# Accumulating the last two layers in the output tensor, with a reordered start and a changed end: a fused block on 8 cores

## Chip, cores, metric

The kernel runs on the 8 cores of one Trainium2 chip (two dies, cores 0 to 3 and 4 to 7). Each core works on 1,024 of the 8,192 tokens, with no traffic between cores. The metric is the device time of the slowest core in microseconds (us).

## What is computed

```python
xn = layernorm(x)                                   # x: 8192 x 2048, f32
a  = (xn @ W_in.T)[:, :4096];  z = silu((xn @ W_in.T)[:, 4096:])
a  = a @ conv_w.T                                   # 4096 x 4096
attn = ((a * D) * z) @ W_out.T                      # -> 2048
h  = relu(xn @ W1.T + b1);  h = relu(h @ W2.T + b2) # 4096, 4096
out = x + attn + (h @ W3.T + b3)                    # 8192 x 2048, f32
```

`W_x`, `W_dt` and `b_dt` of the reference feed nothing that reaches the output.

## The kernel before

Every matrix product is split into a 2 by 2 grid of blocks and is done with seven block products in place of eight (products 5, 2, 1, 3, 4, 6, 7 in that order), whose operands are sums and differences of blocks. VectorE (DVE) forms these sums of weights (`w_sum`, `o_sum`) and of activations (`f_sum`, `new_forms`, `tile_form`), and combines the products, which TensorE (PE) leaves in PSUM. ScalarE (ACT) takes snapshots of PSUM and applies the nonlinearities. GpSimd (POOL) issues the stores and part of the loads, SyncE (SP) the loads of X and of the weights. Each engine has one list of instructions in a fixed order (`Line.do`), with waits on semaphores (`Line.need`).

There are five feature-major layers (`FM`: WX, WZ, W1, WC, W2), 16 pairs of output blocks each (index `g` from 0 to 79), whose results go through DRAM tensors X1S, ZS, H1S, GS, H2S. Then come two token-major layers (`TM`: WO with `si` 0 and W3 with `si` 1), in four chunks of columns each (`x` from 0 to 7). A chunk has the seven products, each in two halves `u` (32 matmuls of 128x256), and gives eight output pieces of 256 tokens by 256 columns (`items`, `n` from 0 to 63): products 3, 4, 6 and 7, two halves each. `o_close(n)` finishes a piece on DVE into one of six ring slots of 256 KB, and `r_store(n)` has POOL store it.

**The residual.** During the first layer POOL loads X tile by tile with `xb_load` (the last load is L526, that of b3 is L522), adds b3 with `xb_add` (L532, 8 tiles) and stores the sum as `XB` (L534). In the WO layer `r_load(n)` (L898, POOL) brings the piece of XB into the ring slot, four pieces ahead (`PREF`), `o_close` adds the product to it, and the sum is stored to `PS`. The W3 layer does the same with PS as its input and OUT as its output. Pieces of products 3 and 4 take one DVE operation (L929). Pieces of products 6 and 7 take two: bank plus running sum (L935), and then plus the loaded piece (L937). The next products in the same PSUM banks wait for these. The first `r_load`s wait for the last store of H2S, since ring and staging buffers share memory.

**The start.** Eight token tiles are normalised (`S`: statistics on DVE L313/L316, `R`: reciprocal deviation on ACT L322/L325, `N` on DVE L335 or `N_act` on ACT L358), transposed on PE (`transposes`, L377, 16 blocks of 128x128 per tile in two PSUM banks `q`), and evacuated (`E`, ACT L398 or DVE L395). Tile 6 is normalised on DVE. PE's order at the end of the start is: transposes of tile 6, the 8 matmuls of `product((0,2))`, transposes of tile 7, `product((0,5))`, `product((1,2))`, `product((1,5))`.

**The end.** The last piece (n = 63) goes through L935 and L937, its store is issued by POOL (L905), POOL waits for the last six stores, and the program closes (L127).

Of the kernel before, what the change touches and what calls it, by code (L numbers as in the profile page):

```python
# [22 lines left out]
CW = 256  # L23

# [21 lines left out]
    dict(w="WO", src="GS", res="XB", dst="PS"),  # L46
    dict(w="W3", src="H2S", res="PS", dst="OUT"),
# [35 lines left out]
def build_program():  # L83
# [17 lines left out]
    for name in ("XB", "PS"):  # L101
        dram[name] = nc.dram_tensor(name, [TC, HID], F32, kind="Internal")
# [19 lines left out]
    c_bs = [ctr(f"bs{i}") for i in range(2)]  # L122
    c_b3 = ctr("b3")
    c_rl = [ctr(f"rl{i}") for i in range(6)]
    c_rs = [ctr(f"rs{i}") for i in range(6)]

    with ExitStack() as ctx:  # L127
# [401 lines left out]
        def xb_add(j):  # L529
            i = j % 2  # L530
            pool.need(tk_bs["b3"], tk_bs[("l", j)])
            t = pool.do(lambda e: e.tensor_tensor(f_f32(4, i), f_f32(4, i), f_f32(5, 0), ALU.add), c_pool)  # L532
            pool.need(t)
            tk_bs[j] = pool.do(lambda e: e.dma_start(dram["XB"][j * 128:(j + 1) * 128, :], f_f32(4, i)),  # L534
                               c_bs[i], 16)
# [171 lines left out]
        for g in range(NG):  # L707
# [435 lines left out]
```

How the kernel before makes its waits and increments, by code:

```python
    def need(self, *toks):  # L65
        for t in toks:
            if t is None:
                continue
            c, v = t
            if self.met.get(c, 0) < v:
                self.met[c] = v
                self.ops.append(lambda e, c=c, v=v: e.wait_ge(c.h, v))
# [1 line left out]
    def do(self, fn, c=None, n=1):  # L74
        if c is None:
            self.ops.append(fn)
            return None
        c.v += n
        self.ops.append(lambda e: fn(e).then_inc(c.h, n))
        return (c, c.v)
```

## Time and profile before

| | us |
|---|---|
| device time, median of 3 runs (1804.3 to 1806.08) | 1805.95 |
| device time of the profiled execution | 1810.24 |
| its span on the slowest core (core 4) | 1808.6 |
| spans of cores 0 to 7 | 1804.3, 1799.3, 1804.9, 1799.2, 1808.6, 1797.7, 1799.1, 1804.1 |
| PE busy on core 4 | 1760.8 |
| DVE, ACT, POOL busy on core 4 | 900.4, 229.1, 212.6 |

A span runs from a core's first instruction to its last. The device time of the profiled execution is 1.6 us more than the longest span. PEld is the loading of weights into PE, which overlaps the matmuls. A wait is put down to what came last before the waiting instruction went on.

### The profile page before, as it was taken

The numbers are of one execution on the slowest core, as the hardware profiler recorded it, in microseconds if no ns is written. First come the engines' busy times: TensorE is split into PE (matmuls) and PEld (weight loads), VectorE is DVE, ScalarE is ACT, GpSimd is POOL, SyncE is SP. The second block draws the span as 40 slices with busy tenths as digits, with TensorE's granted clock in tenths as the row PEclk, the third lists the DMA queues.
The fourth block names the chain that finished last, engine by engine and source line by source line (L and its number), as shares of the span: only waits on it lengthen the run. The fifth ranks groups of instructions, "written<-read, shape, count | busy, mean of one in ns | idle before, by whom it ended". The sixth has DMA issues, their size and how long they took to land.

```text
span 1808.6 us, 24736 instructions; the slowest of 8 cores (1797.7 to 1808.6 us)
## 1 busy us (share of the span) xinstructions
PE 1760.8 (97%) x9911; PEld 977.2 (54%) x9984; DVE 900.4 (50%) x1137; ACT 229.1 (13%) x355; POOL 212.6 (12%) x265
## 2 busy tenths in 40 slices
PE   3999999999999999999999999999999999999998
PEld 2444444444444444444444444444445788888887
DVE  7744444444444674444444743333333654466443
ACT  4111122222222200000000011111111000000000
POOL 0123220000000000000000000000000122212221
PEclk8999999999999999999999999999999999999999
DMA  9566653333347534333345733223337755885532
GB/s 290 179 231 210 229 182 136 140 134 112 139 146 263 172 118 140 127 113 118 132 140 183 259 117 107 91 97 113 117 117 244 224 191 176 268 261 187 166 115 71
DMA packets 58015, 296.33 MB, mean 164 GB/s; under 512 B 7600, under 2 KB 7600, under 8 KB 40368
## 3 DMA queue, kind: packets, MB, share of 16 engines
q1 hardware_dynamic: 29376, 167.79, 28.9%
q0 software_dynamic: 28240, 126.89, 19.7%
q8 instruction: 81, 1.33, 0.3%
q14 instruction: 30, 0.25, 0.0%
q10 hardware_dynamic: 288, 0.08, 0.0%
HBM read 227.62 MB, written 67.11 MB: 163 GB/s over the span
## 4 chain that ended last, share of the span: by engine, by line
PE 90%; DVE 4%; DMA 3%; issue 1%; POOL 0%; ACT 0%; DVEq 0%; SPq 0%; POOLq 0%; ACTq 0%
PE ps L293 72%; PE ps L867 18%; DVE sF L240 2%; DMA sM<-XB 1%; DVE sST L313 1%; DVE sW L240 1%; DMA PS<-sM 1%; DMA H2S<-sM 1%; DMA sF<-X 1%; POOL sM L898 0%; PE ps L377 0%; DVE sM L335 0%; DVE sM L584 0%; DVE sM L562 0%; DVE sM L929 0%
## 5 line engine op out<-in xcount | busy, mean ns | idle before, releaser
L293 PE MATMUL ps<-sF,sW 128*128 128x512 bf16 (+1 forms) x6199 | 1352.7, 379 | 5.7 <-ACT sF L398 0.8
L293 PEld LDWEIGHTS ps<-sF,sW 128*128 128x128 f16 x6272 | 613.6, 98 | 743.4 <-issue 6.2
L240 DVE TENSOR_TENSOR sW<-sW 128x1024 f16<-128x1024 f16 (+1 forms) x480 | 442.6, 954 | 174.5 <-DMA sW<-W 129.8
L867 PE MATMUL ps<-sW,sF 128*128 128x256 f16 x3584 | 394.5, 273 | 6.3 <-DVE sM L929 3.0
L867 PEld LDWEIGHTS ps<-sW,sF 128*128 128x128 bf16 x3584 | 351.0, 98 | 49.9 <-issue 8.3
L557 DVE TENSOR_TENSOR sM<-ps,sM 128x512 f32<-128x512 f32 x80 | 55.4, 692 | 321.1 <-ACT sM L552 321.1
L613 DVE TENSOR_TENSOR sM<-ps,sM 128x512 f32<-128x512 f32 (+1 forms) x160 | 110.2, 690 | 118.8 <-PE ps L293 118.6
L552 ACT ACTIVATE sM<-ps 128x512 f32<-128x512 f32 x80 | 47.8, 598 | 602.6 <-PE ps L293 579.0
L240 DVE TENSOR_TENSOR sF<-sF 128x2048 bf16<-128x2048 bf16 (+2 forms) x94 | 104.3, 1176 | 0.5 <-DMA sF<-H1S 0.5
L594 ACT ACTIVATE sM<-sM,sCN 128x512 bf16<-128x512 f32 x64 | 46.2, 724 | 243.0 <-DVE sM L613 242.9
L562 DVE TENSOR_TENSOR sM<-ps,sM 128x512 f32<-128x512 f32 x80 | 55.0, 688 | 22.9 <-PE ps L293 22.9
L584 DVE SCALAR_TENSOR_TENSOR sM<-ps,sCN,sM 128x512 bf16<-128x512 f32 x32 | 23.9, 751 | 68.2 <-PE ps L293 68.2
L594 ACT ACTIVATE sM<-ps,sCN 128x512 bf16<-128x512 f32 x64 | 44.1, 689 | 104.6 <-PE ps L293 104.5
L625 POOL DMA_DIRECT2D H2S<-sM x16 | 11.5, 717 | 364.9 <-ACT sM L594 364.9
L625 POOL DMA_DIRECT2D GS<-sM x16 | 11.6, 726 | 351.0 <-DVE sM L584 351.0
L911 ACT ACTIVATE sM<-ps 128x512 f32<-128x512 f32 x16 | 9.5, 598 | 339.1 <-PE ps L867 339.0
L929 DVE TENSOR_TENSOR sM<-ps,sM 128x512 f32<-128x512 f32 x32 | 21.8, 690 | 45.2 <-PE ps L867 41.0
L377 PE MATMUL ps<-sID,sM 128*128 128x128 bf16 x128 | 14.4, 300 | 28.0 <-DVE sM L335 26.9
L916 DVE TENSOR_TENSOR sM<-ps,sM 128x512 f32<-128x512 f32 x16 | 10.9, 691 | 61.2 <-ACT sM L911 61.2
L905 POOL DMA_DIRECT2D OUT<-sM x32 | 22.9, 715 | 140.8 <-DVE sM L929 107.0
L532 POOL TENSOR_TENSOR sF<-sF 128x2048 f32<-128x2048 f32 x8 | 36.7, 4583 | 2.7 <-DMA sF<-X 2.7
L905 POOL DMA_DIRECT2D PS<-sM x32 | 22.9, 715 | 108.5 <-DVE sM L929 86.2
(38 smaller groups left out, 316.4 us busy)
## 6 DMA issues: line engine op xcount, KB each, us to landing
sW<-W SPq DMA_DIRECT2D x48, 1024.0 KB, 8.3
sW<-WC SPq DMA_DIRECT2D x32, 1024.0 KB, 8.1
sW<-WX SPq DMA_DIRECT2D x32, 512.0 KB, 6.4
sW<-WZ SPq DMA_DIRECT2D x32, 512.0 KB, 4.7
sW<-W SPq DMA_DIRECT2D x32, 512.0 KB, 4.5
sW<-WO SPq DMA_DIRECT2D x16, 1024.0 KB, 8.2
X1S<-sM POOLq DMA_DIRECT2D x16, 512.0 KB, 6.3
sF<-X POOLq DMA_DIRECT2D x8, 1024.0 KB, 8.8
```

The lines of the kernel that those rows point to most:

```text
L240: return line.do(lambda e: e.tensor_tensor(out, a, b, ALU.subtract if sub else ALU.add), c)
L293: return e.matmul(ps[bank][:], sW[:, c0 + k * 128:c0 + (k + 1) * 128], rhs[:, k * TH:(k + 1) * TH], start=st0, stop=last, skip_group_check ...
L532: t = pool.do(lambda e: e.tensor_tensor(f_f32(4, i), f_f32(4, i), f_f32(5, 0), ALU.add), c_pool)
L552: tk_s2[g] = act.do(lambda e: e.activation(e_buf(g % 2), ps[b][:], AF.Copy, bias=0.0, scale=1.0), c_act)
L557: tk_d[g] = dve.do(lambda e: e.tensor_tensor(e_buf(g % 2), ps[a][:], e_buf(g % 2), ALU.add), c_dve)
L562: tk_e[g] = dve.do(lambda e: e.tensor_tensor(e_buf(g % 2), ps[c][:], e_buf(g % 2), ALU.subtract), c_dve)
L584: tk_o[(g, blk)] = dve.do(lambda e: e.scalar_tensor_tensor(dst, src, d_of(p, half), dst, ALU.mult, ALU.mult), c_dve)
L594: fn = lambda e: e.activation(dst, src, AF.Relu, bias=bias_of(st, p, half), scale=1.0)
L613: t = dve.do(lambda e: e.tensor_tensor(out, ps[bank][:], e_buf(g % 2), ALU.add), c_dve)
L625: lambda e: e.dma_start(d, stg(g % 3).rearrange("p (b t) -> p b t", b=4)), c_st[g % 3], 16)
L867: return e.matmul(ps[bank][:, lo:lo + CW], lhs[:, k * TH + tp * 128:k * TH + (tp + 1) * 128], w[:, k * CW:(k + 1) * CW], start=start, stop ...
L905: tk_rst[n] = pool.do(lambda e: e.dma_start(dst, ring(i).rearrange("p (b i) -> p b i", b=2)), c_rs[i], 16)
```

## The change

X is copied to OUT by eight DMAs from DRAM to DRAM, issued by ACT at g = 3, 7, ..., 31; XB, PS, POOL's additions and all `r_load`s are gone. Pieces are stored with an accumulating DMA (`accum_op=ALU.add`, POOL) onto OUT, in both layers; a store of the W3 layer waits for the store of the same piece in the WO layer. There are seven ring slots, and a slot is free once its last store has landed (`ring_free`). In the WO layer pieces of products 3 and 4 are copied by ACT, and those of 6 and 7 take one DVE addition. In the W3 layer b3 comes from a small buffer that SP fills once per chunk, and DVE adds it: for products 3 and 4 in the one operation, for 6 and 7 to the running sum ahead of the wait for the product. The last two pieces (n = 62, 63) read OUT back (`res_load`, SP), add it ahead of the wait too, and are stored plainly by SP.

In the start, tile 6 is normalised on ACT, tile 7 in two halves on DVE (`norm_halves`), `E(4, 0)` comes after `R(7)`, and `product((0,2))` comes after the transposes of tile 7 and several DVE operations.

```diff
+        def norm_halves(j):
+
+            sbase = j * 32
+            for q in (1, 0):
+                dve.need(tk_rstd[j], tk_x[j], tk_tr[j - 4])
+                tk_norm[j] = dve.do(lambda e, q=q: e.tensor_scalar(
+                    xtm(j)[:, q * 1024:(q + 1) * 1024], xt(j)[:, q * 1024:(q + 1) * 1024],
+                    sST[:, sbase + 24:sbase + 25], sST[:, sbase + 27:sbase + 28],
+                    ALU.subtract, ALU.mult), c_dve)
+                tk_half[(j, q)] = tk_norm[j]
...
+            pe.need(tk_id)
             for q in ((0, 1) if j < 4 else (1, 0)):
+                pe.need(tk_half.get((j, q), tk_norm[j]))
...
+        negmean_dve(6)
         N(5)
         transposes(5)
         R(6)
+        N_act(6)
+        S(7)
         E(4, 1)
+        R(7)
         E(4, 0)
-        S(7)
-        N(6)
+        transposes(6)
         E(5, 1)
-        R(7)
+        w_sum(0, 2)
         E(5, 0, dve)
-        transposes(6)
-        w_sum(0, 2)
-        for si in range(3):
-            form[(si, 2)], form_tok[(si, 2)] = xn["11"], [tk_evac["11"][-1]]
-        product((0, 2), 0, 2, 1, 0, [])
-        N(7)
+        norm_halves(7)
         transposes(7)
         E(6, 1)
         E(7, 1)
@@ -485,15 +502,17 @@
         gran[10] = gran[11] = tk_norm[7]
         load_ready(-1, 5)
         w_sum(0, 5)
+        E(6, 0, dve)
+        for si in range(3):
+            form[(si, 2)], form_tok[(si, 2)] = xn["11"], [tk_evac["11"][-1]]
+            form[(si, 5)], form_tok[(si, 5)] = xn["22"], [tk_evac["22"][-1]]
         w_sum(1, 2)
-        E(6, 0, dve)
         w_sum(1, 5)
-        for si in range(3):
-            form[(si, 5)], form_tok[(si, 5)] = xn["22"], [tk_evac["22"][-1]]
         E(7, 0, dve)
         for t in range(4):
             tile_form(1, t)
         w_sum(0, 1)
+        product((0, 2), 0, 2, 1, 0, [])
         product((0, 5), 0, 5, 0, 0, [])
...
-        def xb_load(j):
-            i = j % 2
-            if j == 0:
-                pool.need(*[tk_norm[x] for x in range(NT)])
-                t = pool.do(lambda e: e.dma_start(f_f32(5, 0), dram["BB3"][:]), c_b3, 16)
-                tk_bs["b3"] = t
-            if j >= 2:
-                pool.need(tk_bs[j - 2])
-            tk_bs[("l", j)] = pool.do(lambda e: e.dma_start(f_f32(4, i), dram["X"][j * 128:(j + 1) * 128, :]),
-                                      c_bx[i], 16)
...
+        def x_copy(j):
+            rows = slice(j * 128, (j + 1) * 128)
+            tk_xc[j] = act.do(lambda e: e.dma_start(dram["OUT"][rows, :], dram["X"][rows, :]), c_bx[j % 2], 16)
...
-            if g < 16 and g % 2 == 1:
-                xb_load(g // 2)
-            if 1 < g <= 16 and g % 2 == 0:
-                xb_add(g // 2 - 1)
+            if g % 4 == 3 and g < 4 * NT:
+                x_copy(g // 4)
...
+        def res_load(n):
+
             si, c, m, u = items[n]
-            i = n % 6
-            if n < 6:
-                pool.need(*[tk_store[x] for x in (L, L - 1, L - 2)])
-            else:
-                pool.need(tk_rst[n - 6])
-            if si == 1:
-                pool.need(tk_rst[n - 32])
+            sp.need(tk_rst[n - 32], tk_rst[n - NRING])
+            src = place("OUT", si, c, m, u)
+            tk_res[n] = sp.do(lambda e: e.dma_start(by_tiles(ring(n % NRING)), src), c_res[u], 16)
+
+        def r_store(n):
+
+            si, c, m, u = items[n]
+            i = n % NRING
+            if is_end(n):
+                sp.need(tk_ro[n])
+                dst = place("OUT", si, c, m, u)
+                tk_rst[n] = sp.do(lambda e: e.dma_start(dst, by_tiles(ring(i))), c_end[u], 16)
+                return
+            pool.need(tk_ro[n], tk_rst.get(n - 32))
             if n == 0:
-                pool.need(tk_bs[6], tk_bs[7])
-            src = place(TM[si]["res"], si, c, m, u)
-            tk_rl[n] = pool.do(lambda e: e.dma_start(ring(i).rearrange("p (b i) -> p b i", b=2), src), c_rl[i], 16)
-
-        def r_store(n):
-            si, c, m, u = items[n]
-            i = n % 6
-            pool.need(tk_ro[n])
-            dst = place(TM[si]["dst"], si, c, m, u)
-            tk_rst[n] = pool.do(lambda e: e.dma_start(dst, ring(i).rearrange("p (b i) -> p b i", b=2)), c_rs[i], 16)
+                pool.need(tk_xc[6], tk_xc[7])
+            dst = place("OUT", si, c, m, u)
+            tk_rst[n] = pool.do(lambda e: e.dma_start(dst, ring(i).rearrange("p (b i) -> p b i", b=2),
+                                                      accum_op=ALU.add), c_rs[i], 16)
...
+        def ring_free(line, n):
+
+            if n < NRING:
+                line.need(*e_start, *[tk_store[x] for x in (L, L - 1, L - 2)])
+            else:
+                line.need(tk_rst[n - NRING])
+
+        b3_used = []
+        tk_b3 = {}
+
+        def b3_load(c):
+
+            sp.need(*(b3_used[-1:] or [*e_start, *[tk_store[x] for x in (L, L - 1, L - 2)]]))
+            c0 = 1024 + NRING * 512
+            src = dram["BB3"][:, :].rearrange("p (h n i) -> p h n i", h=2, n=NCH)[:, :, c, :]
+            tk_b3[c] = sp.do(lambda e: e.dma_start(sM[:, c0:c0 + 2 * CW].rearrange("p (h i) -> p h i", h=2), src),
+                             c_b3, 16)
+
         def o_close(n):
             si, c, m, u = items[n]
-            r = ring(n % 6)
+            r = ring(n % NRING)
             bank = ps[OB["A" if m in (3, 6) else "B"][u]][:]
+            tok = tk_pe[("o", si, c, m, u)]
+            half = {3: 0, 4: 1, 6: 1, 7: 0}[m]
+            if m in (3, 4) and si == 0:
+                act.need(tok)
+                ring_free(act, n)
+                tk_ro[n] = act.do(lambda e: e.activation(r, bank, AF.Copy, bias=0.0, scale=1.0), c_act)
+                return
             if m in (3, 4):
-                dve.need(tk_pe[("o", si, c, m, u)], tk_rl[n])
-                tk_ro[n] = dve.do(lambda e: e.tensor_tensor(r, bank, r, ALU.add), c_dve)
+                dve.need(tok, tk_b3[c])
+                ring_free(dve, n)
+                tk_ro[n] = dve.do(lambda e: e.tensor_tensor(by_tiles(r), by_tiles(bank), b3_at(half), ALU.add), c_dve)
                 return
-            out = fbuf(u) if m == 6 else e_buf(u)
-            dve.need(tk_pe[("o", si, c, m, u)], ot[("e", u)], ot.get(("f", u)) if m == 6 else None)
-            if n < 8:
-                dve.need(*e_start)
-            t = dve.do(lambda e: e.tensor_tensor(out, bank, e_buf(u), ALU.add), c_dve)
-            dve.need(t, tk_rl[n])
-            tk_ro[n] = dve.do(lambda e: e.tensor_tensor(r, out, r, ALU.add), c_dve)
-            if m == 6:
-                ot[("c22", u)] = t
-                ot[("f", u)] = tk_ro[n]
-            else:
-                ot[("c11", u)] = tk_ro[n]
+            base, bt = e_buf(u), ot[("e", u)]
+            if si == 1:
+
+                if m == 6:
+                    ring_free(dve, n)
+                base = r if m == 6 else e_buf(u)
+                dve.need(ot[("e", u)], tk_b3[c], ot.get(("c22", u)) if m == 7 else None)
+                bt = dve.do(lambda e, base=base: e.tensor_tensor(by_tiles(base), by_tiles(e_buf(u)), b3_at(half), ALU.add), c_dve)
+                b3_used.append(bt)
+                if is_end(n):
+                    dve.need(bt, tk_res[n])
+                    bt = dve.do(lambda e: e.tensor_tensor(r, r, e_buf(u), ALU.add), c_dve)
+                    base = r
+            dve.need(tok, bt)
+            ring_free(dve, n)
+            tk_ro[n] = dve.do(lambda e: e.tensor_tensor(r, bank, base, ALU.add), c_dve)
+            ot[({6: "c22", 7: "c11"}[m], u)] = tk_ro[n]
...
-                n = 8 * x + i
-                o_close(n)
-                r_store(n)
-                if n + PREF < len(items):
-                    r_load(n + PREF)
+                if is_end(8 * x + i + 2):
+                    res_load(8 * x + i + 2)
+                o_close(8 * x + i)
+                r_store(8 * x + i)
...
-        for n in range(len(items) - 6, len(items)):
-            pool.need(tk_rst[n])
+        for n in range(len(items) - NRING, len(items)):
+            (sp if is_end(n) else pool).need(tk_rst[n])
```

## Rows read from the trace of the kernel before

**Rows 1.** The page, busy time by engine (core 4).
```profile
PE 1760.8 (97%) x9911; PEld 977.2 (54%) x9984; DVE 900.4 (50%) x1137; ACT 229.1 (13%) x355; POOL 212.6 (12%) x265
```

**Rows 2.** Spans and mean granted TensorE clock by core.
```profile
core 1: 1799.3 us, clock 0.999
...
core 4: 1808.6 us, clock 0.993
...
core 7: 1804.1 us, clock 0.999
```

**Rows 3.** PE's waits, core 4, whole span: us in total, times, longest.
```profile
PE ps L867 <- DVE sM L929: 3.0, 2, 2.5
PE ps L867 <- DVE sW L240: 2.0, 1, 2.0
PE ps L867 <- DVE sM L937: 1.1, 2, 0.7
```

**Rows 4.** PE's waits, core 7, from 1000 us to the end.
```profile
PE ps L867 <- DVE sW L240: 1.9, 1, 1.9
PE ps L293 <- DVE sF L240: 1.3, 1, 1.3
```

**Rows 5.** Timeline, core 4, 37 to 64 us: start, duration, operation, idle before.
```profile
37.49 1.34 DVE L335 TENSOR_SCALAR sM<-sW,sST 128x2048 bf16<-128x2048 f32 x1
...
38.91 25.49 SPq L223 DMA_DIRECT2D sW<-WX  x6
39.08 1.86 PE L377 MATMUL ps<-sID,sM 128*128 128x128 bf16 x16 [2.13 <-DVE sM L335]
...
40.74 3.62 PE L293 MATMUL ps<-sF,sW 128*128 128x512 f16 x8
...
45.68 0.69 DVE L395 CAST sF<-ps 128x1024 f16<-128x1024 bf16 x1 [2.00 <-PE ps L377]
...
46.40 16.38 PE L293 MATMUL ps<-sF,sW 128*128 128x512 f16 x72 [0.82 <-ACT sF L398]
...
63.56 0.81 PE L293 MATMUL ps<-sF,sW 128*128 128x512 f16 x3 [0.78 <-DVE sM L557]
```

**Rows 6.** Timeline, core 4, 19 to 31 us: normalising one tile on ACT.
```profile
27.42 2.10 ACT L358 ACTIVATE sM<-sF,sST 128x2048 bf16<-128x2048 f32 x1
```

**Rows 7.** PE's timeline, core 7, 0 to 75 us.
```profile
39.99 1.87 PE L377 MATMUL ps<-sID,sM 128*128 128x128 bf16 x16 [2.13 <-DVE sM L335]
...
63.78 11.60 PE L293 MATMUL ps<-sF,sW 128*128 128x512 f16 x53 [0.78 <-DVE sM L557]
```

**Rows 8.** Windows, core 5: length, busy by engine, PEclk, DMA share, GB/s.
```profile
38.60:41.20 2.60, 2.60 (x19) 2.05 (x20) 2.60 (x4) 1.02 (x1) 0.00 (x0) 0.50 0.98 296
```

**Rows 9.** Timeline, core 4, 1590 to 1620 us, end of the WO layer.
```profile
1600.16 0.69 DVE L937 TENSOR_TENSOR sM<-sM 128x512 f32<-128x512 f32 x1 [4.76 <-DMA sM<-XB]
...
1606.37 0.69 DVE L937 TENSOR_TENSOR sM<-sM 128x512 f32<-128x512 f32 x1 [2.64 <-DMA sM<-XB]
```

**Rows 10.** Windows, core 4, behind that place.
```profile
1618.50:1621.80 3.30, 3.30 (x18) 2.38 (x16) 3.30 (x4) 0.00 (x0) 0.00 (x0) 0.50 0.49 189
1622.00:1625.00 3.00, 3.00 (x30) 2.70 (x28) 2.34 (x4) 0.00 (x0) 0.00 (x0) 1.00 0.00 0
```

**Rows 11.** Timeline, core 4, the end.
```profile
1797.36 0.69 DVE L935 TENSOR_TENSOR sM<-ps,sM 128x512 f32<-128x512 f32 x1 [1.94 <-PE ps L867]
...
1800.86 0.69 DVE L935 TENSOR_TENSOR sM<-ps,sM 128x512 f32<-128x512 f32 x1 [1.94 <-PE ps L867]
1801.72 0.69 DVE L937 TENSOR_TENSOR sM<-sM 128x512 f32<-128x512 f32 x1 [0.17 <-DVE sM L935]
1802.97 0.72 POOL L905 DMA_DIRECT2D OUT<-sM  x1 [2.78 <-DVE sM L937]
```

**Rows 12.** Line 127, core 4: POOL's closing drain, min/median/max ns.
```profile
L127 POOLq DRAIN  x1: 2523/2523/2523, 1805.6 to 1805.6; - x1
```

**Rows 13.** Stores of L905, core 4, issued 1779 to 1801 us.
```profile
DMA to landing us min/median/max: 2.5/2.6/3.7
```

**Rows 14.** The same, issued 1578 to 1600 us.
```profile
DMA to landing us min/median/max: 8.6/14.6/20.2
```

More of the change, by code:

```diff
@@ L23 @@
 CW = 256
+NRING = 7
 BLK = {"11": 0, "22": 1, "12": 2, "21": 3}
@@ L45 @@
 TM = [
-    dict(w="WO", src="GS", res="XB", dst="PS"),
-    dict(w="W3", src="H2S", res="PS", dst="OUT"),
+    dict(w="WO", src="GS"),
+    dict(w="W3", src="H2S"),
 ]
@@ L100, in build_program @@
         dram[name] = nc.dram_tensor(name, [128, 4 * 16 * TH], BF16, kind="Internal")
-    for name in ("XB", "PS"):
-        dram[name] = nc.dram_tensor(name, [TC, HID], F32, kind="Internal")
     sp, pool, pe, dve, act = Line(), Line(), Line(), Line(), Line()
@@ L121, in build_program @@
     c_bx = [ctr(f"bx{i}") for i in range(2)]
-    c_bs = [ctr(f"bs{i}") for i in range(2)]
     c_b3 = ctr("b3")
-    c_rl = [ctr(f"rl{i}") for i in range(6)]
-    c_rs = [ctr(f"rs{i}") for i in range(6)]
+    c_res = [ctr(f"res{i}") for i in range(2)]
+    c_end = [ctr(f"end{i}") for i in range(2)]
+    c_rs = [ctr(f"rs{i}") for i in range(NRING)]
     with ExitStack() as ctx:
@@ L158, in ring, with b3_at, by_tiles @@
         def ring(i):
-            return sM[:, 2048 + i * 512:2048 + (i + 1) * 512]
+            return sM[:, 1024 + i * 512:1024 + (i + 1) * 512]
+        def b3_at(half):
+            c0 = 1024 + NRING * 512 + half * CW
+            return sM[:, c0:c0 + CW].unsqueeze(1).broadcast_to([128, 2, CW])
+        def by_tiles(ap):
+            return ap.rearrange("p (b i) -> p b i", b=2)
         tk_cn = act.do(lambda e: e.dma_start(sCN[:], dram["CONST"][:]), c_k[0], 16)
@@ L364, in build_program @@
         tk_neg = {}
+        tk_half = {}
         tk_tr = {}
@@ L512, in late_forms @@
                     form[(si, m)], form_tok[(si, m)] = form[(0, m)], form_tok[(0, m)]
-        tk_bs = {}
-        tk_ba = {}
-        def xb_load(j):
-            i = j % 2
-            if j == 0:
-                pool.need(*[tk_norm[x] for x in range(NT)])
-                t = pool.do(lambda e: e.dma_start(f_f32(5, 0), dram["BB3"][:]), c_b3, 16)
-                tk_bs["b3"] = t
-            if j >= 2:
-                pool.need(tk_bs[j - 2])
-            tk_bs[("l", j)] = pool.do(lambda e: e.dma_start(f_f32(4, i), dram["X"][j * 128:(j + 1) * 128, :]),
-                                      c_bx[i], 16)
[L529 to L535, printed above, removed]
+        tk_xc = {}
+        def x_copy(j):
+            rows = slice(j * 128, (j + 1) * 128)
+            tk_xc[j] = act.do(lambda e: e.dma_start(dram["OUT"][rows, :], dram["X"][rows, :]), c_bx[j % 2], 16)
         tk_s2, tk_d, tk_e, tk_c22, tk_c11 = {}, {}, {}, {}, {}
@@ L775, in build_program @@
             if si == 2 and p == 8:
-                bg = [tk_bs[6], tk_bs[7], tk_ba.get(7)]
+                bg = [tk_norm[j] for j in range(6)]
                 load_blk(3, "22", bg)
@@ L876, in build_program @@
         items = [(si, c, m, u) for si in range(2) for c in range(NCH) for m in (3, 4, 6, 7) for u in range(2)]
-        tk_rl, tk_ro, tk_rst = {}, {}, {}
-        ps_stored = []
+        tk_ro, tk_rst = {}, {}
         def place(name, si, c, m, u):
@@ L884, in place, with is_end @@
             return dram[name][r0:r0 + 256, c0:c0 + CW].rearrange("(b p) i -> p b i", b=2)
-        def r_load(n):
+        def is_end(n):
+            return len(items) - 2 <= n < len(items)
+        tk_res = {}
+        def res_load(n):
             si, c, m, u = items[n]
-            i = n % 6
-            if n < 6:
-                pool.need(*[tk_store[x] for x in (L, L - 1, L - 2)])
-            else:
-                pool.need(tk_rst[n - 6])
-            if si == 1:
-                pool.need(tk_rst[n - 32])
-            if n == 0:
-                pool.need(tk_bs[6], tk_bs[7])
-            src = place(TM[si]["res"], si, c, m, u)
-            tk_rl[n] = pool.do(lambda e: e.dma_start(ring(i).rearrange("p (b i) -> p b i", b=2), src), c_rl[i], 16)
+            sp.need(tk_rst[n - 32], tk_rst[n - NRING])
+            src = place("OUT", si, c, m, u)
+            tk_res[n] = sp.do(lambda e: e.dma_start(by_tiles(ring(n % NRING)), src), c_res[u], 16)
         def r_store(n):
             si, c, m, u = items[n]
-            i = n % 6
-            pool.need(tk_ro[n])
-            dst = place(TM[si]["dst"], si, c, m, u)
-            tk_rst[n] = pool.do(lambda e: e.dma_start(dst, ring(i).rearrange("p (b i) -> p b i", b=2)), c_rs[i], 16)
+            i = n % NRING
[5 more added lines that the diff above has]
+            pool.need(tk_ro[n], tk_rst.get(n - 32))
+            if n == 0:
+                pool.need(tk_xc[6], tk_xc[7])
+            dst = place("OUT", si, c, m, u)
+            tk_rst[n] = pool.do(lambda e: e.dma_start(dst, ring(i).rearrange("p (b i) -> p b i", b=2),
+                                                      accum_op=ALU.add), c_rs[i], 16)
         def o_snap(si, c, u):
@@ L967, in build_program @@
         o_sum(0, 0, 1, sum_slots[0][2])
-        PREF = 4
         def finish_pairs():
@@ L1003, in build_program @@
             phase_oa(x)
-            if x == 0:
-                for n in range(PREF):
-                    r_load(n)
+            if si == 1:
+                b3_load(c)
             for u in range(2):
```

1 line of the change is left out of this document (removed).

## Prediction

> **What bounds the kernel now.** First the page: PE is busy for 1760.8 of 1808.6 us [rows 1]. So only three things can give time back: what keeps PE from starting, what makes it wait, and what follows its last matmul. The spans by core come next, since the slowest core sets the time. They fall into two kinds: some cores end near 1799 us, others at 1804 to 1809 [rows 2]. PE's waits tell the kinds apart. Core 4 waits 3.0 + 2.0 + 1.1 = 6.1 us in the last two layers [rows 3]. Core 7 waits 1.9 us there and 1.3 us at a change of layers before it [rows 4]; core 1 has no such wait. The timeline at the end of the WO layer names the source: L937 on DVE waits for pieces of XB (4.76 and 2.64 us) [rows 9]. The layer's closing sums queue behind it on DVE, and PE waits for those. On core 4 the gaps were followed by a stretch in which PE's granted clock was 0.50 (1.2 GHz): 18 matmuls in 3.3 us where 30 fitted in 3.0 us soon after at 1.00 [rows 10]. At the later rate 18 take 1.8 us, so this cost 1.5 us more.
>
> **Start.** Before, PE does the transposes of tile 6 at 39.08, then eight matmuls in 3.62 us at the low clock, and only then the transposes of tile 7. DVE therefore gets to the last evacuation at 45.68, and from there it works without a pause up to the sum that PE waits for at 63.56 [rows 5]. In the new order I move each step by the durations of these rows, on core 4's clock:
> - The statistics and tile 5 stay, but for one tiny operation ahead of tile 5 (some 0.3 us). Normalising tile 6 goes to ACT (2.1 us [rows 6] for DVE's 1.34 [rows 5]), from about 35.0 to 37.1.
> - PE's two halves of tile 6 (1.86 / 2 = 0.93 each) now wait for banks that ACT empties, one evacuation of 1.0 us each around `R(7)`: 38.2 to 39.1 and 39.7 to 40.6.
> - DVE has finished tile 7's first half by 39.7 and its second by 40.3 (1.34 / 2 each), so tile 7 goes through PE at 40.6 to 42.5, with nothing ahead of it. The last evacuation starts at 42.7 in place of 45.68, and DVE's row of work moves by 3.0 us.
> - PE then does `product((0,2))`. If the clock rises when it did before, part of the eight matmuls is slow (0.45 us each) and the rest fast (16.38 / 72 = 0.23 [rows 5]). On core 7 everything is 0.9 us later (39.99 for 39.08 [rows 7]), so this product runs 43.4 to about 45.8, the 72 matmuls end at 62.2, and the matmul that stood at 63.78 [rows 7] starts there. **Gain 1.6 us.** Bounds: 0.4 if all eight are slow, 3.0 if the clock rises early and DVE's 3.0 us is all that limits.
>
> Could the transposes fail to raise the clock? On core 5 PE was kept busy for 2.60 us at PEclk 0.50 with 19 instructions, of which only three were matmuls [rows 8], and its clock rose right after; 16 transposes had carried most of it. The Trainium skill says otherwise (TensorE: Matmul & The Clock Gate, Part 4: PE-mode transpose): transposes do not count as busy in the way matmuls do. By that rule the rise would move with the first matmul, and it is a rival below.
>
> **First layers.** POOL loses eight loads, additions and stores; ACT gains eight DMA issues, one per four pairs, behind its work for a pair; it idles long before each snapshot. Moved bytes are the same or fewer. PE has no wait there on any core, and I cost all of this at 0. If a copy held ACT up for longer than the three products (some 5 us) between a snapshot's input and its user, PE would wait for the excess, eight times over.
>
> **Last two layers.** The loads go, and with them what L929 and L937 wait for. In the WO layer DVE loses 8 of its 12 closing operations per chunk: four move to ACT and four are dropped, 8 x 0.69 = 5.5 us off DVE. The W3 layer keeps its count. So the waits in the last two layers should go: **6.1 us and the slow stretch's 1.5 on core 4, 1.9 us on core 7**. What is late next is a slot of the ring. Piece 8x+7 needs the store of piece 8x, seven half products before; a half product is 1800.86 - 1797.36 = 3.5 us [rows 11], so that store has 24.5 us, and PE feels it only when more work is used up, at some 30 us. No row shows an accumulating store. From below it costs what a plain one does: 2.5 to 3.7 us in quiet [rows 13], 8.6 to 20.2 us while the H2S blocks are loaded [rows 14]. From above I take twice that, since it reads and writes OUT: 7.4 and 40.4 us. I take values near the plain rows, 4.5 and 18, because the wait under load is for other transfers. Then no slot is late.
>
> The 1.3 us of core 7 [rows 4] stay: they come from the blocks of H1S, which the change does not touch.
>
> **End.** Before: from the start of the last L935 (1800.86) to the end (1808.6) are 7.8 us: two additions with a gap, POOL waking (1801.72 + 0.69 to 1802.97, 0.56 us), the store landing 2.5 us later [rows 11, 13], then POOL's drain of 2.52 us [rows 12], then 0.5 us of closing. After: one addition (0.69), SP waking (0.08 us, as after DVE's 37.49 + 1.34 to 38.91 [rows 5]), a landing of 2.5, and the closing 0.6. That is 3.9 us. POOL's drain is off the path, as POOL's own last store is piece 61. Its product ends 7.0 us before the last one, so it is issued at 1800.86 - 7.0 + 0.69 + 0.56 = 1795.1; landing after 4.5 us, with the drain it ends at 1802.2, before SP's 1804.7. The read back and the b3 additions of the last piece fit into the 3.5 us that DVE has ahead of it (2 x 0.69). **Gain 3.9 us**, or 2.7 if SP's store lands after 3.7 us.
>
> **The sum.** Core 7: 1804.1 - 1.9 - 1.6 - 3.9 = 1796.7 us. Core 4: 1808.6 - 6.1 - 1.5 - 1.6 - 3.9 = 1795.5. Core 1: 1799.3 - 1.6 - 3.9 = 1793.8. Core 7 is the slowest, and with the 1.6 us around the span (1810.24 - 1808.6) the time is 1798.3 us. The profiled execution was 4.3 us above the median of 1805.95, by core 4's mishaps. The median fits core 7's 1804.1 + 1.6 = 1805.7, so against it the change is -7.6 us, -0.42%.
>
> **Rivals.**
> 1. *The accumulating store lands late.* One price, the landing time of piece 61's store, decides at the end: up to about 6.5 us it is hidden, and each us beyond is a us. Core 7 gets back to its old span at 6.5 + (1804.1 - 1796.7) = 13.9 us and is slower by more than 0.2% from 17.5 us. With the 20.2 us of the loaded row it gives 1798.3 + 13.7 = 1812.0. For it: reading and writing DRAM in one transfer is unseen here. Against: the quiet row, 2.5 us, even doubled is 7.4. Half way, 10 us, gives 1801.8.
> 2. *The losses move, and do not go.* DVE's waits at the end of the WO layer come under DMA traffic that stays. If the ring or the sums are late there by as much as before, 1.9 us come back: 1800.2.
> 3. *The clock rises later in the start.* If only matmuls raise it, it moves with the first of them, on core 7 from 40.74 + 0.91 = 41.65 to 43.4; the gain falls from 1.6 to 0.8 us: 1799.1. Against: core 5's nineteen [rows 8]. This is what the Trainium skill's page named above would lead to.
> 4. *A copy blocks ACT.* Eight times 1 us gives 1806.3, no change.
>
> **Numbers.** A measurement of this kernel tells about 0.2% (3.6 us) from no change: faster is below 1802.3, slower above 1809.6. My forecast 0.62; rival 1 0.13 (of that 0.05 above 1809.6, 0.02 between, 0.06 below 1802.3); rival 2 0.11; rival 3 0.08; rival 4 0.06 (0.04 no change, 0.02 worse). Faster 0.62 + 0.06 + 0.11 + 0.08 = 0.87, less 0.03 for a sum of several small misses: 0.84. Same 0.09, slower 0.07. The range: down to 1795.0 (the clock's 1.4 us more, core 7's 1.3 us not recurring, and some 0.6 us at the end), up to 1802.5 (start 1.2, end 1.2, waits 1.9 back).
>
> **What the profile will show.** PE's waits in the last two layers near 0 on cores 4 and 7; `sM<-XB` gone; tile 7's transposes right behind tile 6's, and the 72-matmul row starting before 46; one DVE addition after the last matmul and an SP store; POOL's drain ended before the program's end. It is wrong if accumulating stores land after more than 7 us in quiet, or 30 under load, if the last landing is still POOL's, or if ACT's copies show as waits of L557 in the first layers.

## The result and the profile after

The changed kernel takes 1795.72 us (median of 5 runs, 1795.59 to 1797.26) where the kernel before takes 1806.08 (median of its five runs beside it). The ratio is 0.9946, with a 95% interval of 0.993 to 0.9962: 0.54% faster. Forecast were 1798.3 us and 0.42%, with a range from 1795.0 to 1802.5. In some executions the cores of a die show a lower granted clock and the time is some per cent or more longer (one of those five took 1936.54 us); ratios and medians by core are taken without them.

The page and the spans by core after, to be set beside [rows 1, 2]:

```profile
PE 1760.5 (98%) x9984; PEld 976.2 (54%) x9984; DVE 877.1 (49%) x1108; ACT 240.5 (13%) x373; POOL 148.9 (8%) x174
```

```profile
core 0: 1791.7 us, clock 1.000
core 1: 1793.3 us, clock 0.996
...
core 4: 1791.4 us, clock 0.996
core 5: 1794.0 us, clock 0.996
...
core 7: 1791.5 us, clock 1.000
```

PE is as busy as before, so nearly all of the gain is time in which PE stood, ahead of, between or behind its matmuls. And the two kinds of cores are gone: the eight spans lie within 2.7 us (1791.3 to 1794.0), where they lay within 10.9. PE's waits over the whole span of core 5, now the slowest, beside [rows 3, 4]:

```profile
PE ps L396 <- DVE sM L341: 25.3, 4, 16.7
PE ps L396 <- ACT sF L417: 2.5, 3, 1.2
PE ps L299 <- DVE sF L246: 0.9, 1, 0.9
PE ps L299 <- DVE sM L560: 0.8, 1, 0.8
```

No line names L868, the matmuls of the last two layers. The 0.9 us under L246 is the wait for the sums of H1S blocks, which core 7 had before [rows 4] and does not have in this execution.

**The start**, from core 5's timeline (19 to 64 us), beside [rows 5, 6]:

```profile
35.18 2.09 ACT L375 ACTIVATE sM<-sW,sST 128x2048 bf16<-128x2048 f32 x1
...
38.32 1.01 PE L396 MATMUL ps<-sID,sM 128*128 128x128 bf16 x8 [0.85 <-ACT sF L417]
...
39.84 2.67 PE L396 MATMUL ps<-sID,sM 128*128 128x128 bf16 x24 [0.51 <-ACT sF L417]
...
42.35 17.74 PE L299 MATMUL ps<-sF,sW 128*128 128x512 f16 x80
43.00 0.69 DVE L414 CAST sF<-ps 128x1024 f16<-128x1024 bf16 x1
...
60.87 3.40 PE L299 MATMUL ps<-sF,sW 128*128 128x512 f16 x15 [0.78 <-DVE sM L560]
```

The prediction's steps can be read off one by one: tile 6 on ACT from 35.2, PE's first half of it at 38.3, the second half and all of tile 7 in one piece of 24 transposes, DVE's last evacuation at 43.0 (42.7 forecast, 45.68 before, both on core 4, whose first transposes stood at 16.65 us where core 5's stand at 16.70). PE still waits 0.78 us for the same sum, so DVE still bounds the start. Measured from the first transposes, which stand where the first tile of X arrives, PE's matmul behind this wait comes at 60.87 - 16.70 = 44.2 us; before, core 7 had 63.78 - 17.56 = 46.2.

**The end**, core 5: the timeline, then line 126 (the closing drains), then how long the two stores by SP took from issue to landing.

```profile
1785.06 1.18 POOL L911 DMA_DIRECT2D OUT<-sM  x1 [1.24 <-DVE sM L971]
...
1788.10 3.88 SPq L905 DMA_DIRECT2D OUT<-sM  x2
...
1790.83 0.69 DVE L979 TENSOR_TENSOR sM<-ps,sM 128x512 f32<-128x512 f32 x1 [1.34 <-PE ps L868]
```

```profile
L126 POOLq DRAIN  x1: 890/890/890, 1789.5 to 1789.5; - x1
```

```profile
DMA to landing us min/median/max: 2.2/2.2/2.2
```

From DVE's last addition to the end are 1794.0 - 1790.83 = 3.2 us, where [rows 11] had 7.8. POOL's drain is over at 1790.4, before the last addition.

### The profile page after: what moved, and what is told of

It reads as the page before. It is cut to its first block, busy times and chain, and to the rows that moved or that the text cites. A ratio compares the mean times of both kernels' runs of the same rounds, so it can differ in the third digit from the quotient of the medians.

```text
span 1794.0 us, 24704 instructions; the slowest of 8 cores (1791.3 to 1794.0 us)
## 1 busy us (share of the span) xinstructions
PE 1760.5 (98%) x9984; PEld 976.2 (54%) x9984; DVE 877.1 (49%) x1108; ACT 240.5 (13%) x373; POOL 148.9 (8%) x174
## 4 chain that ended last, share of the span: by engine, by line
PE 95%; DVE 2%; DMA 2%; issue 1%; ACT 0%; DVEq 0%; SPq 0%; ACTq 0%; POOLq 0%
PE ps L299 73%; PE ps L868 22%; DMA sF<-H1S 1%; DVE sST L319 1%; DMA sF<-X 1%; DVE sF L246 1%; ACT sF L417 0%; DVE sW L246 0%; PE ps L396 0%; DVE sM L560 0%; DVE sST L322 0%; DVE sM L341 0%; DVE sM L979 0%; DVE sM L565 0%; ACT sST L328 0%
## 5 line engine op out<-in xcount | busy, mean ns | idle before, releaser
L246 DVE TENSOR_TENSOR sW<-sW 128x1024 f16<-128x1024 f16 (+1 forms) x480 | 441.2, 951 | 164.9 <-DMA sW<-W 125.4
L868 PE MATMUL ps<-sW,sF 128*128 128x256 f16 x3584 | 391.6, 273 | 0.0
L868 PEld LDWEIGHTS ps<-sW,sF 128*128 128x128 bf16 x3584 | 350.7, 98 | 41.0
L246 DVE TENSOR_TENSOR sF<-sF 128x2048 bf16<-128x2048 bf16 (+2 forms) x94 | 104.3, 1175 | 2.8 <-DMA sF<-H1S 2.1
L911 POOL DMA_DIRECT2D OUT<-sM x62 | 73.4, 1209 | 294.9 <-DVE sM L962 120.1
L593 ACT ACTIVATE sM<-ps 128x512 bf16<-128x512 f32 x32 | 19.1, 597 | 121.0 <-PE ps L299 121.0
L628 POOL DMA_DIRECT2D X1S<-sM x16 | 11.6, 723 | 232.2 <-DVE sW L246 232.2
```

The source lines that it names most:

```text
L246: return line.do(lambda e: e.tensor_tensor(out, a, b, ALU.subtract if sub else ALU.add), c)
L628: lambda e: e.dma_start(d, stg(g % 3).rearrange("p (b t) -> p b t", b=4)), c_st[g % 3], 16)
L868: return e.matmul(ps[bank][:, lo:lo + CW], lhs[:, k * TH + tp * 128:k * TH + (tp + 1) * 128], w[:, k * CW:(k + 1) * CW], start=start, stop ...
```

## The experiments

On two of the chips used (that of e1 to e4, and that of e9 to e11) cores 0 to 3 had a mean granted clock of 0.98 to 0.995 in the kernel before and in every other kernel, and set the time there. Kernels on these chips are compared on cores 4 to 7. Where a table gives a core's span, it is the median over the kernel's timed executions.

### The three parts, taken singly

`e1_start` is the kernel before with the new start: `norm_halves` and the new order of calls, nothing else. `e3_start_back` is the changed kernel with the old order. `e2_end_back` takes the changed end away:

```diff
         def is_end(n):
-            return len(items) - 2 <= n < len(items)
+            return False
```

`e4_residual` takes both away, so that OUT as accumulator is left.

> The kernel before with the new start alone; residual, stores and end as before. Theory (three gains that add up): every core loses 1.2 to 2.7 us ahead of the matmul that waits for DVE near 60 us (that matmul stands 44.2 us behind the first transposes in place of 45.4 to 46.9), and nothing later moves: time 1804.0 us, ratio 0.9988. PE's waits in the last two layers stay at 2 to 6 us on some cores, and the end stays at 7.9 us behind the last matmul. Rival (waits later take the gain back, or grow with it): 1806, ratio 1.000.

> The changed kernel with the old order of the start. Theory: 1.2 to 2.7 us slower than the changed kernel on each core, 1797.8 us, ratio to before 0.9955; no waits of PE in the last two layers, 3.5 us behind the last matmul. Rival (the start gives nothing to the slowest core): 1795.8, ratio 0.9943.

> The changed kernel with the last two pieces stored like the others: accumulating, by POOL, nothing read back. Theory: from PE's last matmul to the end it takes one addition 0.7, POOL waking 0.6, a landing of 2.5 to 3.5, POOL's drain 2.5 and 0.5 of closing, 6.9 to 7.9 us in place of 3.5: 1799.6 us, ratio 0.9968. Rival (the drain is no cost of its own, only the saved addition and waking count): 1797.3, ratio 0.9955.

> The changed kernel with the old start and the old kind of last stores: what is left of the change is OUT as accumulator, with the copies of X, b3 on DVE and ACT's copies. Theory: it saves the waits of PE in the last two layers on the cores that had them, 2 to 6 us, and at the end one addition: slowest core 1800 to 1801, time 1802.0 us, ratio 0.9978. Rival (less DRAM traffic shortens other waits as well, such as the one at the change from WC to W2): 1800 or less, ratio under 0.9967.

| us | core 4 | 5 | 6 | 7 | mean | ratio of times, interval |
|---|---|---|---|---|---|---|
| before | 1802.7 | 1801.4 | 1803.3 | 1801.7 | 1802.3 | |
| e1_start | 1801.7 | 1798.4 | 1801.6 | 1799.5 | 1800.3 | 0.9985, 0.9966 to 1.0004 |
| e4_residual | 1799.2 | 1801.3 | 1800.3 | 1800.9 | 1800.4 | 0.9944, 0.9922 to 0.9966 |
| e2_end_back | 1797.8 | 1797.4 | 1798.5 | 1798.6 | 1798.1 | 0.994, 0.9917 to 0.9964 |
| e3_start_back | 1795.0 | 1796.3 | 1796.5 | 1798.2 | 1796.5 | 0.9928, 0.9901 to 0.9954 |

The ratios are those of whole times, set by cores 0 to 3, and their intervals are as wide as one part, so I read the means. The start gives 2.0 us onto the kernel before (e1; by the scatter between executions 0.4 to 3.8) and 2.3 onto the residual (e2 against e4; 1.1 to 3.0). The end gives 3.9 (e3 against e4; 2.8 to 4.8). The residual gives 1.8 (0.8 to 3.4). So each part is a gain, and the parts sum to the expected 2, 4 and 2 us within this scatter. The changed kernel itself was not run on this chip. The 10 us by which the changed kernel's whole time is shorter are more than these 8, which are means: the residual takes most from the cores that were slow. In e1_start the matmul that waits near 60 us stands 44.2 us behind the first transposes on five cores, as expected, and 44.3 to 45.5 on cores 2, 3 and 6, and the end stays at 7.9 (8.1 on core 6). The waits of PE late in the kernel are still there on core 4:

```profile
PE ps L880 <- DVE sW L240: 1.6, 1, 1.6
PE ps L880 <- DVE sM L942: 1.4, 1, 1.4
```

In e4_residual core 4 has none, and the end (from PE's last matmul) takes 6.8 to 7.4 us in e2 and e4, where the kernel before takes 7.9. So 0.5 to 1.1 us of what the residual gives lie in the end, the rest in the waits. The expected 6.9 to 7.9 us came out for wrong reasons: on core 5 of e2 POOL's last stores land after 4.2 to 4.4 us, where I had 2.5 to 3.5, and the drain takes 1.05 us, where I had 2.5.

The rival for e4 was that less DRAM traffic shortens other waits too. On these cores nothing speaks for it: 1800.4 is what the theory gave. By the whole time the rival's condition is met (0.9944, below its 0.9967), and the ratios of e2 and e3 are below the expected ones as well. The granted clock accounts for that: cores 0 to 3 had a mean of 0.9874 in the kernel before and in e1, and of 0.9903, 0.9894 and 0.9906 in e4, e2 and e3. 0.9903 for 0.9874 is some 5 us, out of the 6.5 by which e4's cores 0 to 3 are shorter. One such stretch, core 0 of e1 and then of e4 (columns as in [rows 8]):

```profile
77.00:90.00 13.00, 13.00 (x51) 5.33 (x49) 6.96 (x9) 1.54 (x3) 6.34 (x4) 0.81 0.66 228
```

```profile
77.00:90.00 13.00, 13.00 (x62) 5.88 (x61) 6.14 (x10) 2.27 (x4) 1.44 (x2) 1.00 0.44 126
```

Here the old residual has POOL's additions and its loads running, and the new one does not. That these lowered the clock is not shown: other such stretches are in both kernels, and no run varied them alone.

### What the end is made of

`e5_end_pool` keeps the read back and the additions ahead of the product, and has POOL issue the last two plain stores:

```diff
             if is_end(n):
-                sp.need(tk_ro[n])
+                pool.need(tk_ro[n])
-                tk_rst[n] = sp.do(lambda e: e.dma_start(dst, by_tiles(ring(i))), c_end[u], 16)
+                tk_rst[n] = pool.do(lambda e: e.dma_start(dst, by_tiles(ring(i))), c_end[u], 16)
...
-            (sp if is_end(n) else pool).need(tk_rst[n])
+            pool.need(tk_rst[n])
```

> The changed kernel, with the last two pieces still read back, added ahead and stored plainly, but by POOL in place of SP. Theory (POOL's drain ends some 5.1 us behind its last DMA issue, whatever that DMA is): last matmul to the end is 0.8 + 0.6 + 5.2 + 0.4 = 7.0 us in place of 3.5, the same as with accumulating last stores; cores 3.5 us slower than the changed kernel's. Rival (a plain store that lands in 2.5 us lets POOL close early): 4.9 us.

Time 1799.58 us, ratio 0.995 (0.9933 to 0.9967), and from the last matmul to the end 5.4 us on six cores, 5.5 and 5.65 on the other two. My theory of a drain that ends a fixed time behind the last issue gave 7.0 and is wrong, the rival's 4.9 is nearer. Core 4's timeline and drain:

```profile
1788.70 0.69 DVE L979 TENSOR_TENSOR sM<-ps,sM 128x512 f32<-128x512 f32 x1 [1.34 <-PE ps L868]
1789.96 0.74 POOL L905 DMA_DIRECT2D OUT<-sM  x1 [2.75 <-DVE sM L979]
```

```profile
L126 POOLq DRAIN  x1: 1053/1053/1053, 1792.6 to 1792.6; - x1
```

The drain still starts when the store has landed (1789.96 + 2.6), but it takes 1.05 us in place of the 2.52 of [rows 12]. So of the end's 4.4 us (7.9 to 3.5), SP in place of POOL is 2.0 (5.4 to 3.5), and the rest is the saved addition with its hand-over (0.9) and a shorter drain (1.5). Why is the drain shorter? POOL no longer computes in the changed kernel. `e11_pool_add` gives it one addition to do, in the first layer:

```diff
+            if g == 8:
+                pool.need(*[tk_norm[x] for x in range(NT)])
+                pool.do(lambda e: e.tensor_tensor(f_f32(4, 0), f_f32(4, 0), f_f32(5, 0), ALU.add), c_pool)
```

> The kernel with the last two stores plain and by POOL (e5_end_pool), and one addition of a 128x2048 f32 tile on POOL in the first layer, whose result nobody reads. Theory (POOL's closing drain takes 2.5 us in a program in which POOL computes, and 1.05 us in one where it only issues): the drain takes 2.5 us again, and the end 6.9 us for 5.4. Rival (the drain's length comes from the DMAs ahead of it): 1.05 us and 5.4.

POOL's groups of work and its drain, core 4:

```profile
L787 POOL TENSOR_TENSOR sF<-sF 128x2048 f32<-128x2048 f32 x1 | 4.6, 4584 | 0.0
```

```profile
L126 POOLq DRAIN  x1: 1053/1053/1053, 1792.1 to 1792.1; - x1
```

In its one execution the addition ran, the drain stayed at 1.05 us and the end at 5.4. So one addition on POOL does not bring the long drain back; eight of them, as in the kernel before, were not tried. The drain is 2.52 us in both kernels with 64 loads and 64 stores on POOL in the last layers (before, e1_start) and 0.5 to 1.05 in all others. Within these it follows the stores. The drains of e6_ring4 and e9_ring5, which have four and five ring slots (see below), and of e10_plain, on cores 6, 4 and 4:

```profile
L126 POOLq DRAIN  x1: 522/522/522, 1803.3 to 1803.3; - x1
```

```profile
L126 POOLq DRAIN  x1: 645/645/645, 1790.1 to 1790.1; - x1
```

```profile
L126 POOLq DRAIN  x1: 727/727/727, 1786.5 to 1786.5; - x1
```

With seven slots it is 0.89 us, so each slot more is 0.12 us, with the same number of stores; plain stores in place of accumulating ones take 0.16 off, and two more stores by POOL (e2, e4, e5) put 0.16 on. A slot brings a semaphore with it and, at the end, one more store that POOL waits for; which of these counts, and whether the 64 loads make up the rest of the 2.52 us, stays open.

### What accumulating costs, and when a slot is late

`e10_plain` drops `accum_op=ALU.add` from the stores by POOL (and with it the adding of x and of the WO layer's part to all but the last two pieces). `e6_ring4` and `e9_ring5` change one number:

```diff
-NRING = 7
+NRING = 4
```

> The changed kernel with plain stores in place of the accumulating ones, so it leaves out the adding of x and of the WO layer's part to the output (all but the last two pieces). It measures the price of accumulating by itself. Theory: POOL's issue takes 0.72 us for 1.18, a landing 2.6 us in quiet for 4.7 and 10 to 17 us for 18 to 28 while H2S is loaded, and as no slot was late before, PE's waits and the time do not change, within 1 us of the changed kernel. Rival (accumulating traffic costs PE time through late weights or blocks): 1.5 us or more faster, with the waits of 0.3 to 0.9 us gone.

> The changed kernel with four ring slots in place of seven. A piece then waits for the store of the piece four half products before, 14 us, where seven slots give 24.5. Theory (landings of 24 to 28 us while H2S is loaded, 4 to 6 us otherwise): the waits appear at the end of the WO layer alone, where DVE waits for landings and PE then stands for 5 to 10 us; time up by that much, 1801 to 1806 us on a chip where the changed kernel takes 1796. Rival (the slot count matters everywhere, or nowhere since PE's slack covers it): 1796, or over 1815.

> The changed kernel with five ring slots: a piece waits for the store five half products before, 17.5 us, where four slots gave 14 and PE stood for 4 to 9 us at the end of the WO layer. Theory (the landing of 18 to 28 us there is what counts, against the slots' time plus some 8 us of slack): the waits shrink by about 3.5 us per slot, to 0 to 5 us, nowhere but there. Rival (a late slot costs nothing as long as DVE has other work): 0.

Landings of the stores by POOL at the end of the WO layer (issued 1560 to 1600 us), one line for each: core 5 of the changed kernel, core 6 of e6_ring4 (to 1610 us), core 4 of e9_ring5, core 4 of e10_plain.

```profile
DMA to landing us min/median/max: 7.9/24.2/28.0
```

```profile
DMA to landing us min/median/max: 9.4/23.2/30.9
```

```profile
DMA to landing us min/median/max: 17.2/25.3/30.7
```

```profile
DMA to landing us min/median/max: 4.9/9.3/12.4
```

And in the quiet last chunk (1768 to 1787 us), core 5 of the changed kernel and core 4 of e10_plain, the latter with POOL's issues at the end of the WO layer:

```profile
DMA to landing us min/median/max: 4.3/4.7/5.6
```

```profile
DMA to landing us min/median/max: 2.5/2.6/4.4
```

```profile
L911 POOL DMA_DIRECT2D OUT<-sM x8: 707/714/722, 1570.7 to 1595.2; - x8
```

Accumulating makes a landing 2.1 us longer in quiet and 9 to 17 us longer under load (medians of 18.2 to 26.3 us on the eight cores of the changed kernel, 8.6 to 9.8 on cores 4 to 7 of e10_plain), and POOL's issue 1.18 us for 0.71. It costs no time of the kernel on cores 4 to 7: there the medians are 1792.8, 1792.2, 1792.4 and 1793.3 us plain (e10_plain), and on the same chip 1792.7, 1793.2, 1792.8 and 1792.6 accumulating with five slots. So the theory holds there and the rival's 1.5 us are not found, though e10_plain's profile has no wait of PE behind 66 us on any core. On cores 0 to 3 the plain kernel is 1.5 us shorter in the mean, over three and four executions that scatter by more and at a changing clock, which tells nothing either way.

With four slots it does cost. PE's waits, core 6 of e6_ring4, from 1560 to 1660 us (there are none from 1420 to 1560 or from 1660 to 1790):

```profile
PE ps L868 <- DVE sM L979: 7.1, 3, 4.8
PE ps L868 <- DVE sW L246: 2.0, 1, 2.0
```

PE waits 4.2 to 9.1 us there on the eight cores, and the time is 1808.13 us, ratio 0.9992 (0.9979 to 1.0005): four slots give back the whole gain. The expected 5 to 10 us of waits were about right, and the expected 1801 to 1806 us too low. Missing in them is the clock. Behind the waits six of the eight cores have a stretch at 0.50, and two of these have a second one, as in [rows 10]; core 6:

```profile
1620.70:1624.00 3.30, 3.30 (x18) 2.35 (x16) 3.30 (x4) 0.00 (x0) 0.00 (x0) 0.50 0.23 97
```

With it the cores fall 6 to 13 us behind an undisturbed core of the changed kernel at this place. With five slots, only core 4 of the cores 4 to 7 waits, 2.0 us, at landings of up to 30.7 us; core 7 has up to 29.3 and no wait. A slot's time of 17.5 us and a free landing of 29.3 leave some 12 us of PE's slack, where I had 8. Seven slots give 24.5, so my estimate is that a landing hurts from some 36 us; no run has a landing that late.

### The start

`e8_product_between` puts the eight matmuls back between the transposes of tiles 6 and 7; `e7_early_d` puts the sum that PE waits for ahead of two weight sums:

```diff
         norm_halves(7)
+        product((0, 2), 0, 2, 1, 0, [])
         transposes(7)
...
-        product((0, 2), 0, 2, 1, 0, [])
         product((0, 5), 0, 5, 0, 0, [])
```

```diff
+                if g == 1:
+                    make_d(g)
                 if 0 < g < NG - 1:
                     w_sum(g + 1, 5)
                     w_sum(g + 1, 2)
-                make_d(g)
+                if g != 1:
+                    make_d(g)
```

> The changed kernel with the eight matmuls of product((0,2)) back between the transposes of tiles 6 and 7, all else of the new start kept. Theory (the start is bound by DVE, whose last evacuation waits for tile 7's transposes): these come 1.8 to 3.6 us later, and the matmul that waits for DVE near 60 us stands 45.9 to 47 us behind the first transposes in place of 44.2. Rival (DVE's list and ACT's share made the gain, the place of the product none): 44.2 to 44.6.

> The changed kernel with the sum that PE waits for near 60 us (make_d of g = 1) put ahead of the two weight sums in DVE's list. Theory: PE's wait of 0.4 to 0.8 us there goes, and the matmul stands 43.4 to 43.8 us behind the first transposes in place of 44.2; the time changes by under 1 us, 0.05%. Rival (PE then waits as long for the weight sums of g = 2 or for the next sum): 44.2 and no change at 200 us.

PE's timeline of e8, core 1:

```profile
16.21 1.87 PE L396 MATMUL ps<-sID,sM 128*128 128x128 bf16 x16 [16.21 <-DVE sM L341]
...
40.14 3.62 PE L299 MATMUL ps<-sF,sW 128*128 128x512 f16 x8
43.55 1.36 PE L396 MATMUL ps<-sID,sM 128*128 128x128 bf16 x16
45.73 16.38 PE L299 MATMUL ps<-sF,sW 128*128 128x512 f16 x72 [0.82 <-ACT sF L417]
62.89 12.46 PE L299 MATMUL ps<-sF,sW 128*128 128x512 f16 x57 [0.78 <-DVE sM L561]
```

The matmul stands 62.89 - 16.21 = 46.7 us behind the first transposes, and 45.3 to 46.4 on the others: the old start's place (45.4 to 46.9). So the start's gain hangs on tile 7's transposes going ahead of the eight matmuls; ACT's share and the halves alone give nothing. Whether the new place of the product would do without these two was not run. Time 1799.26, ratio 0.995 (0.9933 to 0.9967).

In e7 the wait of 0.4 to 0.8 us near 60 us is gone, and core 0 waits instead a little later:

```profile
42.08 21.14 PE L299 MATMUL ps<-sF,sW 128*128 128x512 f16 x96
63.53 11.81 PE L299 MATMUL ps<-sF,sW 128*128 128x512 f16 x54 [0.32 <-DVE sM L616]
```

By core it keeps 0.5 us at most, and the ratio of 0.9939 (0.9918 to 0.9961) cannot be told from the changed kernel's. So it is not shown to be faster, and none of the experiments pointed to a version that is.

## Why the prediction came out as it did

**The slowest core.** The prediction had core 7 at 1796.7; the slowest is core 5 at 1794.0. Core 7 before had 17.6 us to its first transposes, then 46.2, then 1732.5 to its last matmul, then 7.9. Core 5 after has 16.7 + 44.2 + 1729.7 + 3.5. Four differences: 0.9 us because X arrived earlier, 2.0 from the start, 2.8 between, 4.4 at the end. The 0.9 us are luck: the first transposes stand at 16.2 to 17.6 us on the cores of the kernel before and at 15.8 to 17.8 on those of the changed one. The 2.7 us between the forecast's 1796.7 and 1794.0 are this 0.9, 0.4 in the start, 0.9 between and 0.5 at the end.

**Start, 1.6 us forecast (0.4 to 3.0).** Right in what moves, small by a little: 2.0 on core 7 (and 2.7 on core 4). The forecast had PE's own matmuls end last, at 62.2 us, but on all eight cores the matmul stands at 44.2 us behind the first transposes, where DVE's sum lets it go. The clock is not what I had wrong. On core 7 of the changed kernel it rose 27.0 us behind the first transposes, as late as the 26.8 of core 7 before: its first four matmuls start 0.43 us apart, the others 0.22. Still PE was early. Core 7, changed kernel:

```profile
41.72 18.08 PE L299 MATMUL ps<-sF,sW 128*128 128x512 f16 x80
...
60.17 6.20 PE L299 MATMUL ps<-sF,sW 128*128 128x512 f16 x28 [0.38 <-DVE sM L560]
```

I had put the eight matmuls at 2.4 us and the other 72 at the 16.38 of the old row [rows 5], which core 7 has too, 18.8 together, for 18.1 measured. The 72 are the mis-sized term: the old row hides stops of PE at its end, too short for the list of waits. The last 4 us of those matmuls, core 7 before and then core 7 of the changed kernel:

```profile
58.90:62.90 4.00, 3.77 (x16) 1.15 (x14) 4.00 (x5) 0.00 (x0) 0.00 (x0) 1.00 0.02 4
```

```profile
55.70:59.70 4.00, 4.00 (x19) 1.66 (x17) 4.00 (x6) 0.10 (x1) 0.00 (x0) 1.00 0.01 4
```

Without these stops (0.7 us in all) the forecast's own steps give 61.5 us for PE, just ahead of DVE's 17.56 + 44.2 = 61.7. As for the clock, it rose 25.1 to 28.3 us behind the first transposes on the cores of the kernel before and 25.0 to 27.0 on those of the changed one. In e1, with the new start too, it was 25.1 to 28.3, so no shift by the new order is shown. Windows of the changed kernel, core 4 (columns as in [rows 8]):

```profile
39.10:41.40 2.30, 2.29 (x22) 2.16 (x23) 2.30 (x5) 1.96 (x3) 0.00 (x0) 0.50 1.04 331
41.50:44.00 2.50, 2.50 (x16) 1.20 (x14) 2.50 (x5) 1.11 (x2) 0.00 (x0) 1.00 0.99 313
```

At 0.50 PE had done transposes only, since core 4's first matmul is at 41.56, and the clock was at 1.00 by 41.5. On cores 1, 2, 5 and 6 too it rose ahead of the first matmul. So transposes alone were enough, and rival 3 is out. The Trainium skill (TensorE: Matmul & The Clock Gate, Part 4: PE-mode transpose) says that the full clock does not engage for transposes. That does not hold here.

**First layers, 0 forecast.** Right. ACT's eight issues take 0.52 us each, the copies land after 9 us, and from 60 to 500 us PE has no wait but the 0.8 us at the start. Rival 4 is out.

**Last two layers, 1.9 us on core 7, 6.1 + 1.5 on core 4.** Right: no core waits more than 0.3 us there, and core 4 has no slow stretch. On core 7 it was worth 2.4 us, 0.5 more than the wait, since behind a wait PE also runs at the pace of DVE's pieces for a while. One reading was too narrow: I named the end of the WO layer as the source, but 3.0 of core 4's 6.1 us fall at that layer's beginning, where a late piece of XB holds DVE up by 1.55 us, and the closing additions that PE then waits for come behind DVE's other sums. Core 4 before:

```profile
1437.52 0.69 DVE L929 TENSOR_TENSOR sM<-ps,sM 128x512 f32<-128x512 f32 x1 [1.55 <-DMA sM<-XB]
...
1445.77 4.42 PE L867 MATMUL ps<-sW,sF 128*128 128x256 f16 x39 [2.50 <-DVE sM L929]
```

The landings were 4.5 and 18 us in my sum and 4.7 and 24 on core 5 in the trace, so the loaded one was mis-sized by a third; I had argued that the time under load is for other transfers, and e10 shows that accumulating makes it 2 to 3 times as long. On core 6 it went beyond the 30 us that I had named as a sign of being wrong (stores of L911, 1560 to 1600 us):

```profile
DMA to landing us min/median/max: 14.2/26.3/31.9
```

PE waits 0.3 us there. So the sign was set too low: by the slots the limit is nearer to 36. Rivals 1 and 2 failed by this margin, not by much: at four slots rival 1's mechanism costs PE 4 to 9 us of waits, though at the end of the WO layer and not at the end of the kernel, where I had priced it.

**The 1.3 us at H1S** were to stay. They stay as a kind, but on other cores: core 7 has none, core 5 has 0.9, and there it loses 1.9 in all, with the slower pace behind the wait, where core 7 before lost 2.3. This is 0.4 us of the 2.7 by which the prediction's span is too long.

**End, 3.9 us.** Measured 4.4 to 4.5. SP's landing is 2.2 us on core 5 where I took POOL's 2.5, and the closing 0.2 where I took 0.6. The steps were right (one addition, SP's waking, POOL's drain off the path), as e5 shows. The drain would have shrunk by 1.5 us in any case, which I did not foresee and which the overlap hides.

## What to carry to other kernels

When one engine is busy 97% of the time, look for what differs between the cores: the slow ones here waited for loads that came back late in two loaded stretches, and the way out was to have nothing to wait for. An accumulating store is such a way if its buffer need not be used again too soon; count the landing under the heaviest traffic, not in quiet, against the slots' time plus the consumer's slack. When you move a row of instructions in a forecast, look inside it first: a merged row can hold stops that will not be there in the new order. At the end of a program, look at which engine's closing work comes last, and give the last store to another.

## What the runs showed of the hardware

- An accumulating store of 256 KB takes 4.6 to 5.4 us to land in quiet and 18 to 26 us in the loaded stretch (medians of the changed kernel's cores), a plain one by POOL 2.6 and 9 (e10_plain); POOL's issue takes 1.18 us for 0.71.
- POOL's closing drain took 2.52 us in the kernel before and 1.05, 0.89, 0.73, 0.65 or 0.52 in others. It grew by 0.12 us with each ring slot from four to seven, and one addition on POOL did not change it.
- The last plain 256 KB stores landed in 2.1 to 3.0 us from SP's issue on the eight cores of the changed kernel (2.2 on core 5), and in 2.6 us or a little more from POOL's (e5_end_pool, core 4: 2.6 and 3.1).
- On five of the changed kernel's cores PE's granted clock rose from 0.50 to 1.00 when PE had run nothing but transposes.
- On cores 1 to 6 of e6_ring4, waits of PE of 4.2 to 9.1 us in all were followed by a stretch at 0.50, and cost more than their own length; on cores 0 and 7, with 8.4 and 6.5 us, the clock stayed.
